# Moving the coupling updates of the first two cycles from GpSimd to VectorE

## The chip, the cores and the metric

One core of a Trainium2 chip runs one program from launch to the last store. The time is the device time of that program in microseconds (us). Three runs of the kernel before took 4038.62, 4039.32 and 4045.77 us, a median of 4039.32.

## The reference

Input x is [16, 1024, 256] in fp32. One layer is computed for each of the 16 sequences ("batches"). First a selective-scan block with 512 channels and 16 states per channel:

```
xr = x @ W_in.T + b_in;  xi, res = split(xr)
xi = silu(causal_conv4(xi) + b_conv)
proj = xi @ W_x.T + b_x;  delta = softplus(proj[:512]);  B, C = the next 16 and 16
h_t = exp(delta*A) * h_{t-1} + delta*B*xi;   y_t = sum over states of h_t*C  (+ D*xi)
x1 = layernorm(x + (y * silu(res)) @ W_out.T + b_out)
```

Then a block of three coupling cycles on x1, each of which uses the `out` of the one before:

```
gf = global_net(mean of x1 over time)            # one number per batch
repeat 3 times:
    tf = coupling_net(out)                       # 256 -> 256 -> 128 -> 64 -> 1, gelu, sigmoid
    coupling = 0.1 + range*(0.7*gf + 0.3*tf - 0.5)*2
    out = out + coupling * twist(out)            # twist = [p_r, -p_i, -o_r, o_i]
result = layernorm(x1 + out)
```

The last line of the cycle is what the change is about: a product, `coupling * out`, and an update, `out +- product` with the two halves of the features exchanged.

## The kernel before

The work is cut into **units**. A unit holds 32 channels times 4 states on the 128 partitions and all 1024 steps of time in the free dimension. A batch has 64 units (a **period**), all batches 1024, and every engine has its own instruction stream in which one loop over the unit number `t` is written out. What an engine does in step `t` besides the unit itself is set by tables of positions within the period (lines 53 to 102); engines run apart from one another as far as semaphores allow. For one unit:

- ScalarE makes `da = exp(delta*A)` in PSUM (L816). There are two `da` buffers, so it waits for the VectorE product, or for the scan where GpSimd makes the product, of unit t-2.
- GpSimd makes `work = u*B` (L1060) from `u_q`, a copy of u that SyncE loads for four units at a time (L400), into one of 7 `work` buffers.
- VectorE runs the scan over time (L987). Then the product with C is made: by VectorE for 38 units of a period (L995), by GpSimd, three steps later in its stream, for the other 26 (L1067, the units in `POOL_AT`).
- TensorE sums the states of the products into `y_sum` (L727), and after every eight units VectorE multiplies `y_sum` by the gate (L967).

Beside the units of batch b run the side tasks of its neighbours: projection, convolution and gates of batch b+1 (TensorE L591, L600, L606; ScalarE L878, L887, L914, L918), delta of the blocks of 16 units to come (TensorE L613, ScalarE L938 to L944, VectorE L1020, GpSimd L1082 for u = delta*xi, which SyncE stores to memory and loads back as `u_q`), and of batch b-1 the output projection, the layernorms (VectorE L955, L959) and the three coupling cycles. ScalarE loads another function table (L752) whenever it goes from exp to gelu, tanh or silu and back.

The cycles of batch b-1 start at positions 16, 31 and 44 of the period (`CYCLE_AT`). In each, TensorE and ScalarE run the network; at position +11 (27, 42, 55) VectorE makes two products, one for each half of time, from the coupling in PSUM and `oT` in SBUF into `big` (L1010). Behind the first two cycles, at position +14 (30 and 45), GpSimd waits for them and makes the update with two instructions (L1075, L1076), each 128x1024 with both operands, `oT` and `big`, in SBUF. They signal `updated`, for which TensorE's first layer of the next cycle waits (L681). The update of the third cycle is made by TensorE in the last sum (L667, L668). For the last batch all of this runs after its last unit, with nothing beside it: the tail.

SyncE's stream is in order too: where it waits for one thing, later transfers stand behind it. So `load_u` (L400) of a step stands behind the load of the next x (L367), which waits for TensorE's last gate projection (L606, position 50).

Of the kernel before, what the change touches and what calls it, by code (L numbers as in the profile page):

```python
# [5 lines left out]
ALU = mybir.AluOpType  # L6
# [59 lines left out]
CYCLES = 3  # L66
F_PER = 10
CYCLE_AT = (16, 31, 44)
# [11 lines left out]
MULT_AT, UPD_AT = 11, 14  # L80
# [31 lines left out]
def by_pool(u):  # L112
    return u % PERIOD in POOL_AT
# [30 lines left out]
def phase_reduced(g):  # L144

    return max(REDUCED[u] for u in range(PHASE * g, PHASE * g + PHASE))
# [70 lines left out]
def build(nc, x, xT, weights, vectors, out):  # L217
# [7 lines left out]
    with ExitStack() as ctx:  # L225
        def sb(name, shape):
            return ctx.enter_context(nc.sbuf_tensor(name, shape, F32))
# [4 lines left out]
        def sem(name):  # L232
            return ctx.enter_context(nc.semaphore(name))
# [16 lines left out]
        oT = sb("oT", [P, 2, SEQ])  # L250
        big = sb("big", [P, 2, SEQ])
# [24 lines left out]
        def v(name, c=0, rows=P):  # L276
            a, _ = V_COLS[name]
            return v_all[0:rows, a + c:a + c + 1]
# [60 lines left out]
        f_prod, updated = sem("coupling_products"), sem("updated")  # L339
# [4 lines left out]
        def couplings(t):  # L344

            period, q = t // PERIOD, t % PERIOD
            return [(f, pos) for f, pos in ((period - 2, q + PERIOD), (period - 1, q)) if 0 <= f < BATCH]
# [601 lines left out]
        @block.vector  # L949
        def _(dve):  # L950
            def moments(ready, st, mv, n, i, bank):

                dve.wait_ge(ready, n + 1)
                for r in range(2):
                    ins = dve.bn_stats(stats[:, i, r, :], banks[:, bank, r * DM:(r + 1) * DM])  # L955
                ins.then_inc(st, 1)
                dve.wait_ge(st, n + 1)
                for r in range(2):
                    ins = dve.bn_aggr(mean_var[:, i, r, :], stats[:, i, r, :])  # L959
                ins.then_inc(mv, 1)  # L960

            def gate(pair):

                slot = pair % 2
                dve.wait_ge(reduced, phase_reduced(2 * pair + 1))
                dve.wait_ge(sq_in[slot], 16 * (pair // 2 + 1))
                dve.tensor_tensor(s_quad[:, slot, :, :], y_sum[:, :].rearrange("p (i t) -> p i t", i=2),  # L967
                                  s_quad[:, slot, :, :], ALU.mult).then_inc(gated, 1)

            dve.wait_ge(v_in_sem, 16)  # L970
            for m, end in BY_VECTOR:
                dve.wait_ge(x_taken, 2 * m + 2)
                dve.tensor_scalar(work[:, m, 0:end], xi[:, 0, m, 0:end], v("w_conv", m * TAPS + TAPS - 1), 0.0,
                                  ALU.mult, ALU.add).then_inc(conv_step, 1)
                for back in range(1, TAPS):
                    dve.wait_ge(conv_step, TAPS * m + back)
                    dve.scalar_tensor_tensor(out=work[:, m, back:end], in0=xi[:, 0, m, 0:end - back],
                                             scalar=v("w_conv", m * TAPS + TAPS - 1 - back), in1=work[:, m, back:end],
                                             op0=ALU.mult, op1=ALU.add).then_inc(conv_step, 1)
            for t in range(FIRST, END):  # L980
                g, j, slot = t // PHASE, t % PHASE, t % WORK
                main = 0 <= t < UNITS
                if main:
                    dve.wait_ge(da_ready, t + 1)
                    dve.wait_ge(dbx_ready, t + 1)
                    dst = work[:, slot, :] if by_pool(t) else da[:, t % 2, :]
                    dve.tensor_tensor_scan(dst, da[:, t % 2, :], work[:, slot, :], 0.0, ALU.mult, ALU.add) \  # L987
                       .then_inc(scanned, 1)
                if t % (2 * PHASE) == 0 and 2 <= g <= 16 * BATCH:
                    gate(g // 2 - 1)  # L990
                if main and not by_pool(t):
                    if t % PERIOD < 2 * PHASE:
                        dve.wait_ge(c_in_[j], 16 * (t // PERIOD + 1))
                    dve.wait_ge(scanned, t + 1)
                    dve.tensor_tensor(work[:, slot, :], da[:, t % 2, :], c_quad[:, j, :], ALU.mult).then_inc(prod_dve, 1)  # L995

                for f, pos in couplings(t):
                    for n in range(4):
                        if pos == O_AT[n] + O_STATS:
                            moments(o_ready, o_stat, o_mv, 4 * f + n, n, BANK_OF["o", f, n])  # L1000
                        if pos == E_AT[n] + O_STATS:
                            moments(e_ready, e_stat, e_mv, 4 * f + n, 4 + n, BANK_OF["e", f, n])
                    for c in range(CYCLES):
                        if pos == CYCLE_AT[c] + MULT_AT:
                            cycle = CYCLES * f + c
                            for half in range(2):
                                cols = slice(half * L, half * L + L)
                                shared = banks[:, BANK_OF["f", f, F_PER * c + 8 + half], :]
                                dve.wait_ge(f_ready, F_PER * cycle + 9 + half)
                                dve.tensor_tensor(big[:, :, cols], shared.unsqueeze(1).broadcast_to([P, 2, L]),  # L1010
                                                  oT[:, :, cols], ALU.mult).then_inc(f_prod, 1)

                m, half = delta_at(t, DELTA_MAX)
                if m is not None:

                    cols = slice(half * L, half * L + L)
                    dve.wait_ge(soft_done, 2 * m + half + 1)
                    if m and half == 0:
                        dve.wait_ge(d_stored, 16 * m)
                    dve.scalar_tensor_tensor(out=delta[:, cols],  # L1020
                                             in0=banks[:, BANK_OF["d", m // DC, 2 * (m % DC) + half], :],
                                             scalar=v("b_x", m % DC), in1=soft[:, cols],
                                             op0=ALU.add, op1=ALU.max).then_inc(delta_ready, 1)
# [3 lines left out]
        def _(pool):  # L1027
# [22 lines left out]
            for t in range(FIRST, END):  # L1050
                if 0 <= t < UNITS:
                    g, j, slot = t // PHASE, t % PHASE, t % WORK
                    copied = g % COPIES
                    if j == 0:
                        pool.wait_ge(uq_in[copied], 16 * (g // COPIES + 1))
                    if t % PERIOD < PHASE:
                        pool.wait_ge(b_in_[j], 16 * (t // PERIOD + 1))
                    if t >= WORK:
                        pool.wait_ge(reduced, REDUCED[t - WORK])
                    pool.tensor_tensor(work[:, slot, :], u_q[:, copied, :], b_quad[:, j, :], ALU.mult) \  # L1060
                        .then_inc(dbx_ready, 1)
                un = t - POOL_LAG
                if 0 <= un < UNITS and by_pool(un):
                    if un % PERIOD < 2 * PHASE:
                        pool.wait_ge(c_in_[un % PHASE], 16 * (un // PERIOD + 1))
                    pool.wait_ge(scanned, un + 1)
                    pool.tensor_tensor(work[:, un % WORK, :], work[:, un % WORK, :], c_quad[:, un % PHASE, :], ALU.mult) \  # L1067
                        .then_inc(prod_pool, 1)

                for f, pos in couplings(t):  # L1070
                    for c in range(CYCLES - 1):
                        if pos == CYCLE_AT[c] + UPD_AT:
                            cycle = CYCLES * f + c
                            pool.wait_ge(f_prod, 2 * cycle + 2)
                            pool.tensor_tensor(oT[:, 0, :], oT[:, 0, :], big[:, 1, :], ALU.add)  # L1075
                            pool.tensor_tensor(oT[:, 1, :], oT[:, 1, :], big[:, 0, :], ALU.subtract).then_inc(updated, 1)  # L1076

                m, half = delta_at(t, U_LAG)
                if m is not None and half == 0:
                    pool.wait_ge(delta_ready, 2 * m + 2)  # L1080
                    pool.wait_ge(xi_ready, 8 * (m // DC) + 2 * (m % DC) + 2)
                    pool.tensor_tensor(u[:, :], delta[:, :], xi[:, (m // DC) % 2, m % DC, :], ALU.mult).then_inc(u_ready, 1)  # L1082
# [57 lines left out]
```

## Time and profile before

| | us |
|---|---|
| median of 3 runs | 4039.32 |
| profiled execution, its time | 4040.28 |
| profiled execution, its span | 4038.5 |
| first period starts (first unit's scan) | 63.6 |
| last scan ends | 3903.4 |
| GpSimd busy | 3644.6 (90%) |
| VectorE busy | 3429.6 (85%) |
| TensorE busy | 3524.4 (87%) |
| ScalarE busy | 2959.0 (73%) |

Between the first scan and the end of the last the 16 periods follow one another, of some 240 us each; 135 us of the span are the tail. Mean durations stand in ns behind the busy time of a group; the idle time of an engine in front of a group is given with what ended it.

### The profile page before, as it was taken

How to read it: one execution, taken by the hardware profiler on the slowest of the kernel's cores; microseconds unless marked ns; L12 is line 12 of the kernel's file. 1: busy time of each engine (PE TensorE's matmuls, PEld its weight loads, DVE VectorE, ACT ScalarE, POOL GpSimd, SP SyncE). 2: the span in 40 equal slices, each digit the busy share in tenths (PEclk: the TensorE clock that was granted, in tenths of full speed). 3: DMA queues.
4: the chain of work that ended last, by engine and by line, in shares of the span. 5: the costliest groups of instructions: out<-in, count | busy, mean ns of one | idle time of the engine just before them, and what ended most of it. 6: DMA issues, size and time to landing. Idle time of an engine off the chain costs nothing. (4 is left out here: it accounts for less than half of the span.)

```text
span 4038.5 us, 51729 instructions
## 1 busy us (share of the span) xinstructions
PE 3524.4 (87%) x18776; PEld 1611.5 (40%) x18776; DVE 3429.6 (85%) x2508; ACT 2959.0 (73%) x3918; POOL 3644.6 (90%) x1604
## 2 busy tenths in 40 slices
PE   7669989899998998989898998989989898897766
PEld 3224353443434344353443434344353443434233
DVE  4988988889898898989889898898989889898861
ACT  4447868778786877868777786877868777785753
POOL 4999999999999999999999999999999999999860
PEclk9779999999999999999999999999999999998888
DMA  5354373543536354373644546454363544546320
GB/s 182 130 175 154 128 230 120 188 152 130 186 130 224 129 191 138 122 229 120 197 148 155 159 152 200 140 187 129 133 218 123 194 149 158 160 138 199 127 86 31
DMA packets 329645, 630.04 MB, mean 156 GB/s; under 512 B 27952, under 2 KB 226608, under 8 KB 329136
## 3 DMA queue, kind: packets, MB, share of 16 engines
q1 hardware_dynamic: 329392, 626.74, 47.0%
q8 instruction: 150, 2.46, 0.3%
q14 instruction: 103, 0.84, 0.1%
HBM read 456.76 MB, written 169.87 MB: 155 GB/s over the span
## 5 line engine op out<-in xcount | busy, mean ns | idle before, releaser
L1060 POOL TENSOR_TENSOR work<-u_q,b_quad 128x1024 f32<-128x1024 f32 x1024 | 2397.3, 2372 | 138.2 <-DMA u_q<-u_scratch 97.1
L816 ACT ACTIVATE da<-delta_q,neg_a 128x1024 f32<-128x1024 f32 x1024 | 1126.3, 1112 | 600.9 <-DVE work L995 430.8
L987 DVE TENSOR_TENSOR_SCAN da<-da,work 128x1024 f32<-128x1024 f32 x608 | 1389.9, 2286 | 151.4 <-ACT da L816 119.7
L1067 POOL TENSOR_TENSOR work<-work,c_quad 128x1024 f32<-128x1024 f32 x416 | 985.2, 2368 | 11.6 <-DVE work L987 11.3
L987 DVE TENSOR_TENSOR_SCAN work<-da,work 128x1024 f32<-128x1024 f32 x416 | 945.9, 2278 | 29.9 <-ACT da L816 28.1
L727 PE MATMUL y_sum<-work,v_all 128*32 128x256 f32 x8192 | 613.3, 399 | 303.3 <-POOL work L1067 190.7
L995 DVE TENSOR_TENSOR work<-da,c_quad 128x1024 f32<-128x1024 f32 x608 | 743.9, 1224 | 28.6 <-DMA c_quad<-bc_scratch 4.6
L752 ACT ACT_TABLE_LOAD x563 | 722.3, 1283 | 14.5 <-DMA v_all<-in_vectors 3.9
L727 PEld LDWEIGHTS y_sum<-work,v_all 128*32 128x32 f32 x8192 | 199.8, 110 | 771.0 <-issue 259.3
L613 PE MATMUL banks<-xi,w_all 128*128 128x512 f32 x1024 | 479.8, 612 | 9.4 <-ACT g_act L797 5.1
L600 PE MATMUL banks<-xi,taps 128*128 128x512 f32 x984 | 453.2, 606 | 0.0
L681 PE MATMUL banks<-oT,w_all 128*128 128x512 f32 x768 | 389.7, 635 | 16.8 <-POOL oT L1076 16.7
L606 PE MATMUL banks<-x_feat,w_all 128*128 128x512 f32 x512 | 278.6, 684 | 27.5 <-DVE big L1010 26.7
L613 PEld LDWEIGHTS banks<-xi,w_all 128*128 128x128 f32 x1024 | 188.2, 192 | 259.4 <-issue 237.4
L634 PE MATMUL banks<-w_all,yg 128*128 128x256 f32 x1024 | 262.6, 402 | 30.8 <-DMA oT<-in_x 30.8
L591 PE MATMUL banks<-x_feat,w_all 128*128 128x512 f32 x512 | 256.0, 636 | 26.5 <-ACT big L787 17.2
L600 PEld LDWEIGHTS banks<-xi,taps 128*128 128x128 f32 x984 | 179.4, 191 | 244.1 <-issue 244.1
L787 ACT ACTIVATE big<-banks,v_all 128x512 f32<-128x512 f32 x336 | 218.9, 685 | 66.8 <-PE banks L681 47.0
L1082 POOL TENSOR_TENSOR soft<-delta,xi 128x1024 f32<-128x1024 f32 x64 | 151.2, 2362 | 112.1 <-DVE delta L1020 112.1
L634 PEld LDWEIGHTS banks<-w_all,yg 128*128 128x128 f32 x1024 | 200.9, 200 | 85.6 <-issue 58.5
L681 PEld LDWEIGHTS banks<-oT,w_all 128*128 128x128 f32 x768 | 136.0, 196 | 197.5 <-issue 183.3
L1010 DVE TENSOR_TENSOR big<-banks,oT 128x1024 f32<-128x1024 f32 x96 | 112.6, 1214 | 93.5 <-PE banks L703 93.5
(86 smaller groups left out, 3270.3 us busy)
## 6 DMA issues: line engine op xcount, KB each, us to landing
delta_q<-delta_scratch SPq DMA_DIRECT2D x256, 512.0 KB, 5.8
u_q<-u_scratch SPq DMA_DIRECT2D x256, 512.0 KB, 6.1
delta_scratch<-delta SPq DMA_DIRECT2D x64, 512.0 KB, 2.9
u_scratch<-soft SPq DMA_DIRECT2D x64, 512.0 KB, 2.9
b_quad<-bc_scratch SPq DMA_DIRECT2D x64, 512.0 KB, 4.7
c_quad<-bc_scratch SPq DMA_DIRECT2D x64, 512.0 KB, 7.1
s_quad<-res_scratch SPq DMA_DIRECT2D x128, 256.0 KB, 4.1
y_scratch<-s_quad SPq DMA_DIRECT2D x128, 256.0 KB, 3.2
```

The source lines that it names most:

```text
L600: mm = pe.matmul(banks[:, bank, to:], taps[:, m, k, :], xi[:, nb % 2, m, half * L + to - s:half * L + L - s], start=k == 3, stop=k == 0)
L606: mm = pe.matmul(banks[:, bank, :], w_in[:, k, DI + m * P:DI + m * P + P], x_feat[:, k, half * L:half * L + L], start=k == 0, stop=k == 1)
L613: mm = pe.matmul(banks[:, bank, :], w_x[:, k, m * P:m * P + P], xi[:, nb % 2, k, half * L:half * L + L], start=k == 0, stop=k == 3)
L634: pe.matmul(half, yg[:, n % 2, k, r * P:r * P + P], w_out[:, k, :], start=k == 0, stop=False)
L681: mm = pe.matmul(shared, w1[:, k, m * P:m * P + P], oT[:, k, half * L:half * L + L], start=k == 0, stop=k == 1)
L727: mm = pe.matmul(y_sum[GROUP * i:GROUP * i + GROUP, cols], fold, work[:, un % WORK, QT * i:QT * i + QT], start=False, stop=done)
L752: nc.scalar.preload_act_table_set(name)
L816: act.activation(da[:, t % 2, :], delta_q[:, slot, :], ACT.Exp, scale=neg_a[:, t % PERIOD:t % PERIOD + 1]).then_inc(da_ready, 1)
L987: dve.tensor_tensor_scan(dst, da[:, t % 2, :], work[:, slot, :], 0.0, ALU.mult, ALU.add) \
L995: dve.tensor_tensor(work[:, slot, :], da[:, t % 2, :], c_quad[:, j, :], ALU.mult).then_inc(prod_dve, 1)
L1060: pool.tensor_tensor(work[:, slot, :], u_q[:, copied, :], b_quad[:, j, :], ALU.mult) \
L1067: pool.tensor_tensor(work[:, un % WORK, :], work[:, un % WORK, :], c_quad[:, un % PHASE, :], ALU.mult) \
```

## The change

VectorE issues the update of cycles 0 and 1 right behind its two products, in step 27 and 42 of the period instead of GpSimd in step 30 and 45. It waits on the semaphore `f_prod` of its own two products first. The two instructions have the same operands and the same `updated` signal as before; GpSimd's are gone, with their wait. The third cycle is as it was.

```diff
@@ -1009,6 +1009,10 @@ (VectorE)
                                 dve.wait_ge(f_ready, F_PER * cycle + 9 + half)
                                 dve.tensor_tensor(big[:, :, cols], shared.unsqueeze(1).broadcast_to([P, 2, L]),
                                                   oT[:, :, cols], ALU.mult).then_inc(f_prod, 1)
+                            if c < CYCLES - 1:
+                                dve.wait_ge(f_prod, 2 * cycle + 2)
+                                dve.tensor_tensor(oT[:, 0, :], oT[:, 0, :], big[:, 1, :], ALU.add)
+                                dve.tensor_tensor(oT[:, 1, :], oT[:, 1, :], big[:, 0, :], ALU.subtract).then_inc(updated, 1)
@@ -1066,14 +1070,6 @@ (GpSimd)
-                for f, pos in couplings(t):
-                    for c in range(CYCLES - 1):
-                        if pos == CYCLE_AT[c] + UPD_AT:
-                            cycle = CYCLES * f + c
-                            pool.wait_ge(f_prod, 2 * cycle + 2)
-                            pool.tensor_tensor(oT[:, 0, :], oT[:, 0, :], big[:, 1, :], ALU.add)
-                            pool.tensor_tensor(oT[:, 1, :], oT[:, 1, :], big[:, 0, :], ALU.subtract).then_inc(updated, 1)
```

## Rows read from the trace of the kernel before

**Rows 1.** The page: busy time of the engines, share of the span, instructions.

```profile
PE 3524.4 (87%) x18776; PEld 1611.5 (40%) x18776; DVE 3429.6 (85%) x2508; ACT 2959.0 (73%) x3918; POOL 3644.6 (90%) x1604
```

**Rows 2.** Busy time by stretch (length, then each engine): one period, the last, the tail.

```profile
1491.50:1733.70 242.20, 219.67 (x1176) 100.81 (x1176) 213.67 (x157) 187.17 (x247) 227.23 (x99) 0.96 0.50 161
3668.20:3903.40 235.20, 165.15 (x984) 75.59 (x984) 210.07 (x154) 155.15 (x204) 222.45 (x97) 0.83 0.40 131
3903.40:4038.50 135.10, 87.09 (x346) 52.09 (x344) 18.02 (x45) 41.71 (x103) 9.43 (x5) 0.85 0.19 57
```

**Rows 3.** GpSimd's waits in 14 periods, 290.9 to 3668.2 (total us, times, longest).

```profile
POOL work L1060 <- DMA u_q<-u_scratch: 92.2, 41, 4.0
POOL soft L1082 <- DVE delta L1020: 68.5, 17, 5.7
```

**Rows 4.** Groups of instructions, whole run, by form.

```profile
L1076 POOL TENSOR_TENSOR oT<-oT,big 128x1024 f32<-128x1024 f32 x32 | 75.6, 2362 | 0.0
L995 DVE TENSOR_TENSOR work<-da,c_quad 128x1024 f32<-128x1024 f32 x608 | 743.9, 1224 | 28.6 <-DMA c_quad<-bc_scratch 4.6 <-DVE da L987 0.5
L977 DVE SCALAR_TENSOR_TENSOR work<-xi,v_all,work 128x1023 f32<-128x1023 f32 x2 | 2.6, 1283 | 0.1
```

**Rows 5.** VectorE right behind cycle 0's products, in order of time (start, us, [idle before]).

```profile
1600.13 2.28 DVE L987 TENSOR_TENSOR_SCAN work<-da,work 128x1024 f32<-128x1024 f32 x1
1607.48 2.30 DVE L987 TENSOR_TENSOR_SCAN da<-da,work 128x1024 f32<-128x1024 f32 x1 [1.61 <-ACT da L816]
1618.09 0.69 DVE L967 TENSOR_TENSOR s_quad<-y_sum,s_quad 128x512 f32<-128x512 f32 x1 [1.39 <-PE y_sum L727]
```

**Rows 6.** The same place in another period: the scan that waited 1.61 above.

```profile
1366.50 2.30 DVE L987 TENSOR_TENSOR_SCAN da<-da,work 128x1024 f32<-128x1024 f32 x1 [0.26 <-ACT da L816]
```

**Rows 7.** ScalarE in order of time behind cycle 0's products.

```profile
1611.13 1.12 ACT L816 ACTIVATE da<-delta_q,neg_a 128x1024 f32<-128x1024 f32 x1 [2.65 <-DVE work L995]
1614.57 1.26 ACT L914 ACTIVATE xi<-banks,v_all 128x512 f32<-128x512 f32 x2 [1.03 <-PE banks L600]
```

**Rows 8.** GpSimd in order of time, pieces from cycle 0's products on.

```profile
1599.18 2.35 POOL L1060 TENSOR_TENSOR work<-u_q,b_quad 128x1024 f32<-128x1024 f32 x1
1608.41 2.38 POOL L1067 TENSOR_TENSOR work<-work,c_quad 128x1024 f32<-128x1024 f32 x1
1655.38 2.38 POOL L1067 TENSOR_TENSOR work<-work,c_quad 128x1024 f32<-128x1024 f32 x1
1666.94 2.41 POOL L1067 TENSOR_TENSOR work<-work,c_quad 128x1024 f32<-128x1024 f32 x1
1696.30 7.03 POOL L1060 TENSOR_TENSOR work<-u_q,b_quad 128x1024 f32<-128x1024 f32 x3 [3.32 <-DMA u_q<-u_scratch]
```

**Rows 9.** VectorE in order of time at cycle 1's products.

```profile
1655.16 2.36 DVE L1010 TENSOR_TENSOR big<-banks,oT 128x1024 f32<-128x1024 f32 x2 [0.66 <-PE banks L703]
1659.75 1.22 DVE L995 TENSOR_TENSOR work<-da,c_quad 128x1024 f32<-128x1024 f32 x1
```

**Rows 10.** ScalarE, then TensorE's weight loads, behind cycle 1's products.

```profile
1661.01 1.12 ACT L816 ACTIVATE da<-delta_q,neg_a 128x1024 f32<-128x1024 f32 x1 [4.98 <-DVE work L995]
...
1685.03 0.16 PEld L727 LDWEIGHTS y_sum<-work,v_all 128*32 128x32 f32 x8 [0.76 <-DVE work L995]
```

**Rows 11.** SyncE: two issues in order of time, and its wait in total.

```profile
1688.66 0.39 SPq L367 DMA_DIRECT2D x_feat<-in_xT  x1
1689.96 0.53 SPq L400 DMA_DIRECT2D u_q<-u_scratch  x1
...
SPq L367 <- PE banks L606: 145.7, 15, 10.3
```

**Rows 12.** The tail in order of time, cycle 0 of the last batch.

```profile
3968.25 2.36 DVE L1010 TENSOR_TENSOR big<-banks,oT 128x1024 f32<-128x1024 f32 x2 [23.14 <-PE banks L703]
3970.68 2.34 POOL L1075 TENSOR_TENSOR oT<-oT,big 128x1024 f32<-128x1024 f32 x1 [67.12 <-DVE big L1010]
3975.46 9.67 PE L681 MATMUL banks<-oT,w_all 128*128 128x512 f32 x16 [7.00 <-POOL oT L1076]
```

## Prediction

> **What bounds the kernel now.** The page's busy shares come first: GpSimd is the busiest engine with 90% [rows 1], so a change that takes 9.4 us a period from it looks like a gain. The busy time by stretch says how near the engines are: in one period of 242.2 us GpSimd has 227.2, TensorE 219.7, VectorE 213.7 [rows 2]. Three engines lie within 6%, so what counts is which of them the others wait for at the two places where the update stands. That is read from the waits.
>
> GpSimd's waits in 14 periods are the first clue: 92.2 us for `u_q` and 68.5 us for `delta`, together 160.7 or 11.5 us a period [rows 3]. The order of time puts a long one of them behind both updates: before unit 56 GpSimd stands 3.32 us until `u_q` lands [rows 8]. That copy was issued at 1689.96, behind the load of x at 1688.66 in SyncE's stream [rows 11]. SyncE waits there for TensorE's gate projection, 15 times in the run and 145.7 us in all [rows 11], once for each batch loaded. And TensorE, in front of that projection, had waited 0.76 us for a VectorE product [rows 10]. So at positions 50 to 56 the order is VectorE, TensorE, SyncE, copy, GpSimd: GpSimd runs ahead and is stopped by the others' pace. What is taken from it at positions 30 and 45 makes these waits longer and moves nothing.
>
> VectorE's own pace in the same stretch is a ring with ScalarE: two `da` buffers, so `da` waits for the product of two units before. At cycle 1 ScalarE stood 4.98 us until the product at 1659.75 was done [rows 10, 9]. Whatever is put in front of that product delays the ring by its full length. At cycle 0 there is some slack: VectorE waited 1.61 us for `da` shortly behind its products and 1.39 us for the gate's sum [rows 5], ScalarE 1.03 us for TensorE [rows 7].
>
> **The change part by part.** All sums are made against the profiled execution's own 4040.3 us, which is 1.0 above the median of the runs.
>
> Removed: GpSimd's 2 instructions in each of 2 cycles. 4 x 2.36 us = 9.4 us a period [rows 4]. It is covered by the waits above, so in 14 full periods (batches 0 to 13, periods 1 to 14) I cost it at nothing; if the cover were gone it would be worth up to 9.4 us a period.
>
> Added: 4 instructions on VectorE a period. No VectorE row of the steady part has both tensor operands in SBUF: its products read the coupling or `da` from PSUM. The nearest rows are the product of the same size at 1.22 us and the prologue's two-operand instruction, all SBUF, at 1.28 us [rows 4]; I take 1.25, so 2.5 us a cycle. The added wait for `f_prod` is for VectorE's own instruction in front, as between scan and product (0.5 us in 608 times [rows 4]), so nothing. No DMA moves, and SyncE's waits do not name `updated`. TensorE's wait for `updated` costs nothing in the periods and none is added: VectorE signals at about the time GpSimd did.
>
> The unknown is whether these instructions wait for GpSimd. The L977 rows fell before GpSimd's main loop (no copies of u existed yet), and since then VectorE never read two SBUF tensors beside it; no row shows it either way. Ends: nothing, or one at a time with GpSimd's, which are 2.36 us each. In the second case the first update waits for the GpSimd instruction in flight, then GpSimd's next one, pending by then, goes, then the second update.
> Cycle 0: VectorE is free at 1600.2 [rows 5], the GpSimd instruction in flight ends at 1599.18+2.35 = 1601.5 [rows 8]: 1.3 + 1.25 + 2.36 + 1.25 = 6.2 us.
> Cycle 1: free at 1655.16+2.36 = 1657.5 [rows 9], GpSimd's ends at 1655.38+2.38 = 1657.8 [rows 8]: 0.2 + 1.25 + 2.36 + 1.25 = 5.1 us.
> Without waiting both are 2.5. I take the upper value: GpSimd's 2.36 us for what costs VectorE 1.22 [rows 4] look like an engine that gets its two operands one after the other through one path, and a second SBUF operand of VectorE has to come from somewhere too.
> The Trainium skill speaks against this change here: "SBUF — State Buffer", section "Who interferes with whom", says that a VectorE instruction with two inputs in SBUF contends with a GpSimd one that reads SBUF, and that the one that comes second is held until the other is through. No run here shows it yet; by that rule the sum is the one of 6.2 and 5.1 us, without it the one of 2.5 and 2.5.
>
> What the slack takes off: at cycle 0 the 1.61 us wait of the scan is up before anything is late; in another period the same wait is 0.26 [rows 6], so about 1.0 on average. Then ScalarE's 1.03 or the gate's 1.39 [rows 7, 5], whichever is less, since both paths lead to the next scan. Together 2.1 us (between 1.3 and 3.0). At cycle 1 nothing: ScalarE's 4.98 us of waiting end with VectorE's product. A period thus grows by (6.2 - 2.1) + 5.1 = 9.2 us; 14 x 9.2 = 129 us. The rest of the period passes it on: GpSimd's dense stretch from unit 56 starts with the `u_q` whose order was followed above.
>
> The last period has no batch to prepare, and GpSimd has fewer waits in it: 222.5 us busy in 235.2 [rows 2]. It gives up 9.4 us there and is held for 4 x 1.25, VectorE takes 11.3 more of its 25 idle: between -4.4 and +6 us, taken as 0.
>
> Tail: the update is a link of a bare chain. GpSimd's pair runs from 3970.68, and TensorE starts at 3975.46, having waited 7.00 us [rows 12]: 4.8 us of it for the pair. VectorE's takes 2.5 with GpSimd idle, so each of 2 cycles gains 2.2: -4.4 us.
>
> Sum: 4040.3 + 129 + 0 - 4.4 = 4164.9; against the median, 4164.
>
> **The rivals.**
> (a) VectorE's two updates go together once the first has started, and only the first waits: 3.8 and 2.7 us, so (1.7 + 2.7) x 14 - 4.4 = +57, 4097 us. For it: VectorE's instructions follow one another with no gap. Against it: so do GpSimd's, and one that is pending has waited longer.
> (b) No waiting at all: (0.4 + 2.5) x 14 - 4.4 = +36, 4076 us. It also is slower, since the place, not the wait, is what hurts. For it: VectorE's scans with one SBUF operand run 2.28 us beside GpSimd without a trace of one.
> (c) GpSimd keeps its turn as long as it has work, and VectorE starts only where GpSimd must wait. At cycle 0 that is soon: without the update GpSimd makes one more L1060, to 1603.9, and then its L1067 (now at 1608.41 [rows 8]) needs the scan that stands behind VectorE's update. 3.7 + 2.5 = 6.2. At cycle 1 it has two instructions before the L1067 now at 1666.94 [rows 8]: from 1657.5 to 1662.4, so 4.9 + 2.5 = 7.4. (4.1 + 7.4) x 14 - 4.4 = +157, 4196 us. The buffers thus bound the wait from above.
> (d) The other side: GpSimd is the bound through the period, as its 90% say, and its waits for `u_q` and `delta` move forward with it. The place that decides is the dense stretch from unit 56, 7 GpSimd products in 7 units; the gain comes if GpSimd gets there earlier, so if the copy for unit 56 lands earlier by more than VectorE's delay. Then 9.4 less 4 x 1.25 in which it is held, 4.4 us, is gained a period: 14 x 4.4 + 4.4 = 66 us, 3974 us (3904 if nothing is held). Against it: GpSimd's wait of 3.32 us at exactly that unit, which must vanish first.
> That the update isn't moved isn't to be feared: both streams are written out by the same tables.
>
> **How the numbers follow.** Forecast 0.45, (a) 0.17, (b) 0.14, (c) 0.10, (d) 0.14. A difference under 0.2% (8 us) can't be told from no change in this kernel. (b) with cycle 0 wholly absorbed and (d) with its gain eaten by VectorE could end there: 0.06 for the same, taken from both; faster 0.13, slower 0.81. The range reaches from below (b) to (c): 4050 to 4200 us, with (d) left out below and little above. The forecast's own range, by the slack (1.3 to 3.0 a period), the first wait (0 to 2.36 in place of 0.2 at cycle 1) and the last period, is 4145 to 4200.
>
> **What would show it.** GpSimd: four fewer instructions a period, and its waits for `u_q` and `delta` up by 5 to 9 us a period. VectorE's new rows: busy 2.5 us for two, or each stretched or started late by up to 2.4 us; under (a) only the first. A GpSimd instruction beside them stretched by 1.25 each. Periods of 249 to 252 us instead of 240 to 242. ScalarE's wait for the product behind cycle 1 up from 4.98 to about 10. In the tail TensorE's wait down from 7.00 to about 4.8. The prediction is wrong if GpSimd's waits in front of unit 56 don't grow, or if periods get shorter.

## The result and the profile after

The changed kernel takes 4183.34 us (median of 4 runs, 4167.27 to 4186.69) against 4040.11 us: 1.0344 of before, 95% interval 1.0315 to 1.0373. Such a ratio is worked out from all the runs on both sides and can differ from that of the medians in the third decimal. The prediction was 4164 us, slower. The profiled execution is the fastest of the four, 4167.27 us with a span of 4165.5, 127.0 us more than before.

First the page's busy time, then the busy time by stretch: one full period, the last period, the tail.

```profile
PE 3567.3 (86%) x18776; PEld 1618.7 (39%) x18776; DVE 3605.2 (87%) x2572; ACT 2962.0 (71%) x3918; POOL 3530.2 (85%) x1540
```

```profile
1784.50:2033.50 249.00, 221.29 (x1176) 99.67 (x1176) 225.73 (x161) 187.27 (x248) 220.19 (x95) 0.96 0.48 157
3793.00:4034.00 241.00, 162.41 (x988) 75.21 (x992) 219.90 (x158) 155.07 (x204) 216.91 (x93) 0.84 0.39 127
4034.00:4165.50 131.50, 87.53 (x344) 52.15 (x342) 22.72 (x49) 41.68 (x103) 0.00 (x0) 0.88 0.20 58
```

These answer to [rows 1, 2]. GpSimd has become less busy and VectorE more: VectorE is now the busier of the two in a period, 225.7 against 220.2 us. The 14 middle periods took 3503.4 us together (289.6 to 3793.0) in place of 3377.3, so 126.1 more or 9.0 each. The last period is 5.8 longer, the tail 3.6 shorter, and what lies before them 1.3 shorter: 126.1 + 5.8 - 3.6 - 1.3 = 127.0.

Where in the period the time went is read from the starts of VectorE's scans, as means of the 14 periods. From the scan of unit 27 to that of unit 42, the stretch with cycle 0's update, they took 60.82 us in place of 57.26; from 42 to 50, with cycle 1's, 34.52 in place of 28.57; the rest of the period 154.9 in place of 155.4. So the delay arises at the two places alone, 3.6 and 5.9 us, and the rest gives 0.5 back.

One other thing changed: TensorE took 46 us more over these periods, at a lower mean granted clock (the column behind GpSimd's busy time, as a share of full speed; before, then after).

```profile
290.90:3668.20 3377.30, 3069.96 (x16464) 1406.93 (x16464) 2989.99 (x2181) 2617.84 (x3450) 3183.35 (x1373) 0.97 0.49 162
289.60:3793.00 3503.40, 3115.95 (x16464) 1414.43 (x16464) 3151.02 (x2237) 2620.91 (x3450) 3083.90 (x1317) 0.95 0.47 156
```

No run separates this from the updates. But a slower TensorE would be felt all through the period, and the stretches away from the two updates did not get longer.

Where VectorE's time went is shown by the two new instructions, first for the whole run (minimum, median and maximum in ns) and then in order of time: cycle 0, cycle 1 of one period, and cycle 1 of another.

```profile
L1014 DVE TENSOR_TENSOR oT<-oT,big x32: 1224/2359/7151, 397.6 to 4124.9; 128x1024 f32<-128x1024 f32 x32
L1015 DVE TENSOR_TENSOR oT<-oT,big x32: 1210/3361/3380, 399.8 to 4126.1; 128x1024 f32<-128x1024 f32 x32
```

```profile
1641.65 2.36 DVE L1014 TENSOR_TENSOR oT<-oT,big 128x1024 f32<-128x1024 f32 x1
1643.93 3.36 DVE L1015 TENSOR_TENSOR oT<-oT,big 128x1024 f32<-128x1024 f32 x1
...
1205.21 1.24 DVE L1014 TENSOR_TENSOR oT<-oT,big 128x1024 f32<-128x1024 f32 x1
1206.37 3.36 DVE L1015 TENSOR_TENSOR oT<-oT,big 128x1024 f32<-128x1024 f32 x1
...
1701.14 7.13 DVE L1014 TENSOR_TENSOR oT<-oT,big 128x1024 f32<-128x1024 f32 x1
1708.19 1.21 DVE L1015 TENSOR_TENSOR oT<-oT,big 128x1024 f32<-128x1024 f32 x1
```

This waiting is no idle time in the profile: it is inside the duration of the instruction. Alone, in the tail, each takes 1.22. With GpSimd at work the first takes 2.36 at cycle 0, and the second 3.36 = 1.22 + 2.14: a whole GpSimd instruction came between. At cycle 1 there are two kinds of pairs. Beside them, GpSimd in order of time (cycle 0, then the two kinds at cycle 1):

```profile
1638.27 7.94 POOL L1064 TENSOR_TENSOR work<-u_q,b_quad 128x1024 f32<-128x1024 f32 x3
1649.58 2.35 POOL L1071 TENSOR_TENSOR work<-work,c_quad 128x1024 f32<-128x1024 f32 x1 [3.36 <-DVE work L987]
...
1203.00 2.37 POOL L1071 TENSOR_TENSOR work<-work,c_quad 128x1024 f32<-128x1024 f32 x1
1205.32 6.61 POOL L1064 TENSOR_TENSOR work<-u_q,b_quad 128x1024 f32<-128x1024 f32 x2
...
1700.22 2.35 POOL L1071 TENSOR_TENSOR work<-work,c_quad 128x1024 f32<-128x1024 f32 x1
1702.53 4.65 POOL L1064 TENSOR_TENSOR work<-u_q,b_quad 128x1024 f32<-128x1024 f32 x2
1715.14 2.37 POOL L1071 TENSOR_TENSOR work<-work,c_quad 128x1024 f32<-128x1024 f32 x1 [7.96 <-DVE work L987]
```

At cycle 0 three instructions take 7.94 us where three took 7.03 before [rows 8]: the one between the updates was held by 0.9. At 1203 VectorE came just as GpSimd's product ended, so only its second update waited. At 1700 GpSimd wasn't held at all: it ran its product and two more, VectorE waited through all three, and got in when GpSimd had nothing left but the product that needs the scan behind the update. That is rival (c), and it happened in 6 of 14 periods. The pairs took 5.63 us on average at cycle 0. At cycle 1 they took 4.51 to 4.59 in 7 periods, 6.52 in one in which VectorE had to wait in front of both updates but got each turn, and 6.67 to 8.28 in the 6 with a missed turn, on average 6.06.

The waits that answer to [rows 3] and [rows 10], [rows 12], all of after (GpSimd, 289.6 to 3793.0; ScalarE at cycle 1; TensorE in the tail):

```profile
POOL work L1071 <- DVE work L987: 174.6, 54, 8.0
POOL work L1064 <- DMA u_q<-u_scratch: 133.8, 42, 5.7
POOL soft L1078 <- DVE delta L1024: 62.6, 16, 5.7
POOL work L1064 <- PE y_sum L727: 24.5, 22, 1.4
POOL work L1064 <- DMA b_quad<-bc_scratch: 22.8, 14, 3.0
...
1712.90 1.12 ACT L816 ACTIVATE da<-delta_q,neg_a 128x1024 f32<-128x1024 f32 x1 [12.50 <-DVE work L995]
...
PE banks L681 <- DVE oT L1015: 9.6, 2, 4.8
```

GpSimd's waits grew from 193.7 us (all of them in these periods, [rows 3] among them) to 418.3, by 16.0 a period, and the largest is nearly new: its products wait for the scan behind the update (7.6 us before, 174.6 after). ScalarE's wait behind cycle 1 is 12.50 us in the period shown, one with a missed turn, and 10.4 on average, where it was 4.4 before.

### The profile page after: what moved, and what is told of

The parts are those of the page before. It is cut to its first block and busy times, and to the rows that moved or that the text cites. A ratio compares the mean times of both kernels' runs of the same rounds, so it can differ in the third digit from the quotient of the medians.

```text
span 4165.5 us, 51729 instructions
## 1 busy us (share of the span) xinstructions
PE 3567.3 (86%) x18776; PEld 1618.7 (39%) x18776; DVE 3605.2 (87%) x2572; ACT 2962.0 (71%) x3918; POOL 3530.2 (85%) x1540
## 3 DMA queue, kind: packets, MB, share of 16 engines
q8 instruction: 150, 2.46, 0.2%
## 5 line engine op out<-in xcount | busy, mean ns | idle before, releaser
L1064 POOL TENSOR_TENSOR work<-u_q,b_quad 128x1024 f32<-128x1024 f32 x1024 | 2427.0, 2398 | 201.9 <-DMA u_q<-u_scratch 137.0
L727 PE MATMUL y_sum<-work,v_all 128*32 128x256 f32 x8192 | 622.4, 403 | 394.4 <-DVE work L995 212.5
L600 PE MATMUL banks<-xi,taps 128*128 128x512 f32 x984 | 469.2, 624 | 0.0
L681 PE MATMUL banks<-oT,w_all 128*128 128x512 f32 x768 | 416.1, 671 | 18.7 <-DVE oT L1015 9.6
L681 PEld LDWEIGHTS banks<-oT,w_all 128*128 128x128 f32 x768 | 145.3, 210 | 214.7 <-issue 187.0
L718 PE MATMUL y_sum<-xi,diag_d 128*32 128x256 f32 x2048 | 173.3, 412 | 24.7 <-DVE s_quad L967 24.4
```

The lines of the kernel that those rows point to most:

```text
L600: mm = pe.matmul(banks[:, bank, to:], taps[:, m, k, :], xi[:, nb % 2, m, half * L + to - s:half * L + L - s], start=k == 3, stop=k == 0)
L681: mm = pe.matmul(shared, w1[:, k, m * P:m * P + P], oT[:, k, half * L:half * L + L], start=k == 0, stop=k == 1)
L727: mm = pe.matmul(y_sum[GROUP * i:GROUP * i + GROUP, cols], fold, work[:, un % WORK, QT * i:QT * i + QT], start=False, stop=done)
```

## Experiments

All ratios are against runs of the kernel before on the same chip.

**No updates at all.** In the changed kernel the update lines are taken out, and TensorE waits for the products.

```diff
-                            pe.wait_ge(updated, (CYCLES - 1) * f + c)
+                            pe.wait_ge(f_prod, 2 * (CYCLES * f + c))
...
-                            if c < CYCLES - 1:
-                                dve.wait_ge(f_prod, 2 * cycle + 2)
-                                dve.tensor_tensor(oT[:, 0, :], oT[:, 0, :], big[:, 1, :], ALU.add)
-                                dve.tensor_tensor(oT[:, 1, :], oT[:, 1, :], big[:, 0, :], ALU.subtract).then_inc(updated, 1)
```

> The updates of cycles 0 and 1 are left out on both engines; TensorE's next layer waits for the products. Theory (GpSimd is not what the periods wait for): the 14 middle periods stay at 240 to 242 us, GpSimd's waits grow by about 9 us a period, only the tail gets shorter, by twice 4.8 us: about 4030 us. Rival (GpSimd is the bound): each period shorter by up to 9.4 us, 4040 - 15 x 9.4 - 10 = about 3890 us; half of that counts for it too.

Measured: 4034.3 us, 0.9970 (0.9955 to 0.9986). The 14 middle periods took 3380.9 us against 3377.3: GpSimd's 9.4 us a period are worth nothing there. Its waits (290 to 3674, the five largest):

```profile
POOL work L1060 <- DMA u_q<-u_scratch: 143.6, 43, 6.1
POOL soft L1074 <- DVE delta L1020: 69.8, 19, 5.7
POOL work L1067 <- DVE work L987: 47.0, 23, 2.8
POOL work L1060 <- PE y_sum L727: 38.1, 28, 2.3
POOL work L1060 <- DMA b_quad<-bc_scratch: 26.5, 14, 2.9
```

With 1.8 us more they sum to 326.8, 133.1 more than before; the removed work is 14 x 9.4 = 131.6. All of it turned into waiting. The gain in the medians, 9 us, is about what the tail gives: 125.4 us in place of 135.1. Rival (d) falls.

**The place alone.** The kernel before, GpSimd's updates kept, and behind VectorE's products four instructions with one SBUF input each, whose results nothing uses.

```diff
+                            if c < CYCLES - 1:
...
+                                for k in range(4):
+                                    ins = dve.bn_stats(filler[:, k, :], w_all[:, k * L:k * L + L])
...
```

> The kernel before with its GpSimd updates, and at positions 27 and 42 behind VectorE's products four more VectorE instructions of 512 elements that read one SBUF tensor each, about 0.7 us each, 2.7 us together, and feed nothing. Theory (the place costs, even with no waiting for GpSimd): cycle 0 hides 2.1 of 2.7, cycle 1 nothing: 14 x 3.3 = 46 us, 4086 us. Rival 1 (only waiting for GpSimd costs, VectorE has 25 us of idle time a period to hide 5.4): 4040 us. Rival 2 (GpSimd is the bound): 4040 us too. If these single-input instructions also wait for GpSimd, their rows show 1 to 2 us each instead of 0.7.

```profile
L1019 DVE BATCH_NORM_STATS2 filler<-w_all 128x6 f32<-128x512 f32 x128 | 78.8, 678 | 0.0
```

Measured: 4085.84 us, 1.0102 (1.0076 to 1.0127), +42 us for +46 expected. The fillers took 0.68 us each, 0.67 to 0.69 in all 128, so these instructions, which read one SBUF tensor, did not wait for GpSimd, and still the kernel is slower. Their rows overlap: four of them take 2.46 us, 4.9 a period, and the 14 middle periods grew by 33.0 us, 2.4 each; 4.9 us more came in the last period. So VectorE's 28 idle us a period [rows 2] hid only half of the 4.9: nearly all of it at cycle 0, whose stretch grew by 0.4 us, and nothing at cycle 1, whose stretch grew by 2.6. Rival 1 and 2 fall, and this is also about the price of rival (b), put at 2.9 a period.

**One cycle at a time.** The update of cycle 0 alone, then of cycle 1 alone, on VectorE.

```diff
+                            if c == 0:
...
-                        if pos == CYCLE_AT[c] + UPD_AT:
+                        if c == 1 and pos == CYCLE_AT[c] + UPD_AT:
```

The edit is to the kernel before: behind the first line stand the other three lines of the change, and the condition below leaves GpSimd the other cycle. In the second run 0 and 1 are exchanged.

> Only cycle 0's update on VectorE, cycle 1's stays on GpSimd. In the changed kernel VectorE's pair of cycle 0 took 2.36 + 3.36 = 5.65 us every time. Theory with my slack of 2.1 us: 14 x 3.6 - 2 = +48 us, 4088 us. Rival (slack of VectorE's 1.61 and 1.39 us waits does not count, each delay is passed on in full): 14 x 5.7 - 2 = +77 us, 4117 us. Rival (it is cycle 1 alone that costs): 4040 us.

> Only cycle 1's update on VectorE. In the changed kernel its pair took 4.6 us in 8 periods and 6.5 to 8.4 in 6. Theory (no slack at cycle 1): 14 x 6.0 - 2 = +82 us, 4122 us, and together with the run that moves cycle 0 alone the sum of the change, +143. Rival (GpSimd's relief pays part of it back once the other update is left on it): clearly less, under 4090 us.

Durations of the updates in the middle periods, cycle 0 alone and then cycle 1 alone:

```profile
L1015 DVE TENSOR_TENSOR oT<-oT,big 128x1024 f32<-128x1024 f32 x14 | 47.1, 3367 | 0.0
L1014 DVE TENSOR_TENSOR oT<-oT,big 128x1024 f32<-128x1024 f32 x14 | 32.8, 2346 | 0.5
...
L1014 DVE TENSOR_TENSOR oT<-oT,big 128x1024 f32<-128x1024 f32 x14 | 67.6, 4829 | 0.5
...
L1015 DVE TENSOR_TENSOR oT<-oT,big 128x1024 f32<-128x1024 f32 x14 | 25.6, 1827 | 0.0
```

Measured: cycle 0 alone 4097.51 us, 1.0132 (1.0104 to 1.0160); cycle 1 alone 4148.55 us, 1.0255 (1.0230 to 1.0281). In the profiled executions the 14 middle periods grew by 47.7 and 91.6 us, 3.4 and 6.5 a period. The pairs took 5.64 and 6.58, so cycle 0 hides 2.2 us of its delay and cycle 1 nothing (0.0). That measures the slack, the term that I had put at 2.1 and 0. Both runs came out slower than expected, by 10 and 27 us; in the second VectorE missed its turn in 10 of 14 periods, where the expected value counted on 6. The parts sum to 139 us in the profiled executions, the whole change to 126. Some 7 of these 13 us are the longer pairs of cycle 1 (6.58 for 6.06); the rest is open.

**One instruction in place of two.** It adds `big` as it stands, so it leaves out the exchange of the halves and the minus sign.

```diff
-                                dve.tensor_tensor(oT[:, 0, :], oT[:, 0, :], big[:, 1, :], ALU.add)
-                                dve.tensor_tensor(oT[:, 1, :], oT[:, 1, :], big[:, 0, :], ALU.subtract).then_inc(updated, 1)
+                                dve.tensor_tensor(oT[:, :, :], oT[:, :, :], big[:, :, :], ALU.add).then_inc(updated, 1)
```

> The changed kernel with each update as one VectorE instruction of 2048 elements, still two SBUF operands; it adds big to oT without the exchange of halves and the sign, so that part of the arithmetic is changed. Theory (what costs is a turn for each VectorE instruction): cycle 0 waits once, 1.1 + 2.3 = 3.4 us in place of 5.65; cycle 1 0.1 + 2.3, or up to 4.8 more where GpSimd keeps its turn, 2.4 to 7.2 in place of 4.6 to 8.4. About 2.3 us less a period each where a second turn was lost: 14 x (2.3 + 1.3) = 50 us less than 4183, 4130 us. Rival (the two engines share the reads and slow each other by the element): no gain, 4183 us.

```profile
1637.67 3.33 DVE L1014 TENSOR_TENSOR oT<-oT,big 128x2048 f32<-128x2048 f32 x1
```

Measured: 4146.23 us, 1.0249 (1.0234 to 1.0265). Cycle 0 took 3.41 us on average (expected 3.4) in place of 5.63. Cycle 1 took 2.3 in 3 periods, 4.2 in one and 6.8 to 7.8 in 10, on average 6.08, no better than before: the one turn that was saved was lost to more missed ones. So 37 us less than the change, for 50 expected; cycle 0's 2.2 us in 14 periods are 31 of them.

**Four instructions in place of two.** Halves of 512 elements.

```diff
+                                for m, op in ((0, ALU.add), (1, ALU.subtract)):
+                                    for h in range(2):
+                                        part = slice(h * L, h * L + L)
+                                        ins = dve.tensor_tensor(oT[:, m, part], oT[:, m, part], big[:, 1 - m, part], op)
...
```

> The changed kernel with each update in four VectorE instructions of 512 elements in place of two of 1024. Theory (turns with GpSimd, bounded by what GpSimd can still do before it needs the scan behind the update: one more instruction at cycle 0, two at cycle 1): cycle 0 1.1 + 4 x 0.7 + 2.2 = 6.1 us in place of 5.65, cycle 1 0.1 + 4 x 0.7 + 2 x 2.2 = 7.3 in place of 6.2 on average; 14 x 1.6 = 22 us more, about 4205 us. Rival (each instruction pays a turn whatever GpSimd has left): 1.1 + 2.8 + 6.6 = 10.5 and 9.5 us, 14 x 8.2 = 115 more, 4298 us. Rival (reads are shared by the element): 4183 us and the small start-up cost of 0.3.

```profile
398.82 2.35 DVE L1010 TENSOR_TENSOR big<-banks,oT 128x1024 f32<-128x1024 f32 x2
401.20 5.79 DVE L1017 TENSOR_TENSOR oT<-oT,big 128x512 f32<-128x512 f32 x4
```

Measured: 4208.41 us, 1.0405 (1.0386 to 1.0424), 4205 expected. Cycle 0 took 5.76 us (in durations of 1.8, 2.8, 0.7, 0.7: two turns, then GpSimd stood), where 6.1 was expected, and cycle 1 7.83 for 7.3, with a missed turn in 11 of 14 periods. That the total fits so well is partly luck. It isn't a turn for each instruction without end: GpSimd needs VectorE's next scan, and that bounds the waiting.

**What decides whether VectorE gets its turn.** At cycle 1 of all runs so far the GpSimd instruction in flight was mostly its product of unit 42; at cycle 0 never.

```diff
-POOL_AT = (..., 33, 36, 42, 44, 49, ...)
+POOL_AT = (..., 33, 36, 41, 44, 49, ...)
```

> The changed kernel with GpSimd making the product of unit 41 in place of unit 42 (VectorE the other one), so that at cycle 1's update a GpSimd instruction of the kind work<-u_q,b_quad is in flight, as at cycle 0, and not a product. So far VectorE got its turn at the end of every such instruction at cycle 0, and behind a product only once in 32 times unless it came in its last 0.2 us. Theory (what is in flight decides): cycle 1's pair is 4.5 to 6.8 us every time, the first update never longer than 3.5 us, no pair over 7 us; about 4175 us. Rival (it is the place in the period or chance): first updates of 5 to 7 us in about 6 of 14 periods as before, 4183 us.

```profile
L1014 DVE TENSOR_TENSOR oT<-oT,big x32: 1224/2370/7203, 400.4 to 4167.0; 128x1024 f32<-128x1024 f32 x32
```

Measured: 4202.61 us, 1.0389 (1.0371 to 1.0406). The theory falls: with an instruction of the other kind in flight VectorE missed its turn in all 14 periods (first updates of 5.8 to 7.2 us). What decides it stays open; mere chance from period to period is unlikely, as 6 of 14 became 14 of 14. The price of the turns fits at the place: cycle 1's pair is 7.5 us on average in place of 6.1, 1.5 more, and the stretch from the scan of unit 27 to that of unit 50 is 1.4 longer than in the changed kernel. The whole fits less well: 14 x 1.5 = 21 us, where the medians differ by 19 and the 14 periods of the two profiled executions by 33.

**The tail alone.** The kernel before, with VectorE's update for the last batch only.

```diff
+                            if c < CYCLES - 1 and f == BATCH - 1:
...
-                        if pos == CYCLE_AT[c] + UPD_AT:
+                        if f < BATCH - 1 and pos == CYCLE_AT[c] + UPD_AT:
```

> The kernel before, with VectorE making the updates for the last batch alone, where GpSimd is idle. Theory: twice 4.8 less 2.5 us, -4.5 us, so 0.1% faster, about 4036 us against 4040; TensorE's wait for the update 4.8 instead of 7.0 us. Rival (the tail's chain runs elsewhere): no change.

Measured: 4039.3 us, 0.9989 (0.9977 to 1.0001): not told from no change. Its profile has TensorE's two waits for the update at 9.6 us together in place of 14.1, the 4.5 us expected, but the tail as a whole is only 1.7 us shorter there, and the runs vary by more.

**The load in front of the copy.** The kernel before with SyncE's load of the next x five steps later, then the same without updates.

```diff
-XFEAT_AT = 48
+XFEAT_AT = 53
```

> The kernel before with SyncE's load of the next x at position 53 instead of 48, behind the two copies of u for units 56 to 63 instead of in front. Theory (GpSimd's dense stretch starts with the copy that stands behind SyncE's wait for TensorE): GpSimd's wait before unit 56 (3.3 us) goes and it starts earlier; if that stretch bounds the period's end, up to 14 x 3.3 = 46 us less, 3995 us. Rival (VectorE and ScalarE's ring sets the pace there and GpSimd's waits only move elsewhere): 4040 us, GpSimd's waits for delta or the reductions up by what the copy's go down.

> The x load at position 53 and, as in the run without updates, none of the updates of cycles 0 and 1. Theory (with the copy early, GpSimd's 9.4 us a period can be of use at last only if GpSimd bounds the end of the period): the same as the x load alone less the tail's 9.6 us. Rival (GpSimd would have been the bound but for the copy): 14 x 9.4 = 130 us less, about 3900 us.

SyncE around position 50 in the run with the load later, and GpSimd's waits there (290 to 3658):

```profile
1676.81 0.53 SPq L400 DMA_DIRECT2D u_q<-u_scratch  x1
...
1681.46 0.55 SPq L400 DMA_DIRECT2D u_q<-u_scratch  x1
1686.52 0.38 SPq L367 DMA_DIRECT2D x_feat<-in_xT  x1
...
POOL soft L1082 <- DVE delta L1020: 69.3, 28, 5.7
POOL work L1060 <- DMA u_q<-u_scratch: 59.5, 29, 3.3
...
POOL work L1067 <- DVE work L987: 26.8, 34, 1.4
```

Measured: 4027.02 us, 0.9959 (0.9946 to 0.9972). The copy no longer stands behind the load [rows 11], GpSimd's waits for copies fall from 92.2 us [rows 3] to 59.5, and the wait before unit 56 is gone. 16 of the 46 us possible came. The rival holds for the rest: GpSimd's wait moved in part to its products, which wait 26.8 us for the scan in place of 7.6. Without updates as well: 4013.8 us, 0.9927 (0.9912 to 0.9943), 13 us less again. In the profiled executions the tail gives 9.3 and the 14 middle periods 3.6. So even then GpSimd's relief is worth some 4 us of 131, and runs that spread over 18 us hardly tell that from nothing.

**The best version.** The load later and the tail's updates on VectorE.

> The kernel before with the x load at position 53 (alone 0.9959 of before) and VectorE's update for the last batch alone (alone 0.9989, not clear of no change). Theory: both add, -16 - 4.5 us, about 4022 us or 0.995 of before, the best version so far. Rival: the tail's part is nothing, 0.996.

Measured: 4019.6 us, 0.9943 (0.9926 to 0.9961), faster than both kernels; the tail's part by itself stays within the uncertainty.

## Why the prediction was right, point by point

- **What bounds the kernel.** Right. GpSimd's 90% were no bound at the two places: taking the updates away altogether left the periods as they were (3380.9 us for 3377.3).
- **VectorE's cost without waiting**, 2.5 us a cycle: right, 2.36 for the pair in the tail, 1.23 + 1.22 less an overlap of the rows.
- **The waiting.** Right in kind. Each of the two instructions waits for GpSimd, and the second for a whole instruction, 14 of 14 times at cycle 0: (a) and (b) fall. The row that I leaned on, GpSimd's 2.36 us for what costs VectorE 1.22, was weak evidence. The Trainium skill ("SBUF — State Buffer", "Who interferes with whom") says that a VectorE instruction with one SBUF input does not contend with GpSimd and one with two does. The trace agrees: fillers with one took 0.68 us undisturbed, updates with two took 2.36 and 3.36 where they need 1.22. But that only the one that comes second is held, as the prediction put it, does not fit the 6 missed turns: there VectorE also waited for GpSimd instructions whose rows start behind its own (1702.53, behind 1701.14).
- **Cycle 0**: 6.2 put, 5.63 measured. The first wait was 1.14 for 1.3, the second 2.14 for 2.36.
- **Cycle 1**: 5.1 put, 6.06 measured, and this term was mis-sized. Its fair part is 4.5, as VectorE mostly came just as GpSimd's instruction ended; but in 6 of 14 periods GpSimd kept its turn, as in (c), at 6.7 to 8.3 us for the 7.4 put there. I had treated as two rivals what alternates from period to period. The 0.6 us too much at cycle 0 and the 1.0 too little at cycle 1 offset each other in part, which is luck.
- **Slack**: 2.1 at cycle 0 and 0 at cycle 1 put; 2.2 and 0.0 measured with one cycle moved at a time, and 2.1 and 0.1 in the whole change, by the stretches of the period (5.63 - 3.56 and 6.06 - 5.95).
- **Sum**: 9.2 us a period put, 9.0 in the profiled execution. The two places took 9.5, and the 0.5 that the rest of the period got shorter is no term of the sum. Last period 0 put, +5.8 measured, at the upper end of its bounds; tail -4.4 put, -3.6 measured. The profiled execution is the fastest, and the median is 16 us above it: by the medians the change costs 143 us, where some 124 were forecast. Those 19 us are not explained. More missed turns in the slower runs could make them, but only one run has a trace.
- **Two signs that did not come.** GpSimd's wait right before unit 56 was to grow by VectorE's delay, and I had named its not growing as what would prove me wrong. It is 3.00 us in place of 3.32, and as the mean of 14 periods 2.8 in place of 2.7. Its waits for `u_q` and `delta` were to grow by 5 to 9 us a period, and grew by 2.6 (133.8 + 62.6 us for 160.7). GpSimd's total waits did grow, by 16.0 a period, but mostly in front of the products behind the two updates: 3.4 us before that of unit 28, 5.7 before that of unit 44 (7.96 us at 1715.14). That this wait keeps GpSimd level with VectorE up to unit 56 is argued, not shown. The run without updates shows the cover by itself: before unit 56 GpSimd waits 2.9 us there too, and the freed time went into the waits before unit 36 (5.2 us in place of 1.8) and before the product of unit 49 (2.8 in place of 0.3). So that GpSimd's work was covered held, and which wait covers it was wrong.

```profile
1747.86 4.68 POOL L1064 TENSOR_TENSOR work<-u_q,b_quad 128x1024 f32<-128x1024 f32 x2 [3.00 <-DMA u_q<-u_scratch]
```

## What to carry to other kernels

An engine's busy share does not say that work taken from it is worth anything: read who it waits for behind the place, and leave out the work to measure it. Moving work onto an engine costs where the others wait for its next instruction, even if it stands idle for 12% of the period, as VectorE did here. A VectorE instruction with two SBUF operands beside a busy GpSimd should be priced, as measured here, as itself plus a GpSimd instruction, and as all that GpSimd has ready at worst; keep one operand in PSUM (VectorE's products of the same size with one there took 1.22 us on average), or leave it where it is.

## What was not expected of the hardware

When VectorE had to wait for GpSimd, GpSimd did not always give way at the end of its instruction. Five of the kernels above have cycle 0's update on VectorE in all periods, and five cycle 1's, with 70 updates each in their middle periods. At cycle 0 VectorE got in every time, having come 1.06 to 1.23 us after the start of the instruction in flight. At cycle 1 it did not in 51 of the 70, and then it waited until GpSimd stood: in the kernel with the product of unit 41, 5.8 to 7.2 us for 1.22 us of work in 14 of 14 periods. Neither the kind of instruction in flight nor how far it had got tells the two apart (1.22 us after the start of the same kind of instruction: in at cycle 0, missed at cycle 1 of that kernel).
